# Cross attention in two layers: the context norm's scale and shift put into the key and value weights, the split of the context moved between engines, the keyless test rewritten, buffers doubled, and the written-out order replaced

## The reference, cut to what matters

```python
# layer 0: causal attention of x on the first 112 context rows that tril lets through
Q = relu(queries @ Wq.T + bq); K = relu(keys @ Wk.T + bk); V = relu(values @ Wv.T + bv)
scores = Q_ @ K_.T / 4
key_mask = sign(abs(sum(keys, -1)));  scores = where(key_mask == 0, NEG, scores)
scores = where(tril == 0, NEG, scores)
out = softmax(scores) * query_mask @ V_ + queries
x = gamma * (out - mean) / (std + EPS) + beta
# layer 1: causal self attention, cross attention on the whole context, and a feed-forward part
result = tgt + selfattention(ln1(tgt)) @ sa_wproj + sa_bproj
xq = ln(result) * ln2_g + ln2_b
xs = ln(src) * ln2_g + ln2_b            # src: the context, 375 rows of each batch
k2, v2 = split(xs @ ed_wkv)
result += softmax(xq @ ed_wq @ k2.T * scale) @ v2 @ ed_wproj + ed_bproj
result += relu(ln3(tgt) @ ff_w1 + ff_b1) @ ff_w2 + ff_b2
```

## Time and profile before

| | |
|---|---|
| three runs | 398.64, 398.82 and 401.52 us |
| median | 398.82 us |
| the profiled execution's own time | 397.9 us |
| its span, first to last instruction | 396.1 us |
| granted TensorE clock, mean | 0.978 of full |
| busy: PE, PEld | 336.6 us (85%), 269.4 us (68%) |
| busy: DVE, ACT, POOL | 242.8 us (61%), 171.4 us (43%), 69.6 us (18%) |
| DMA | 13.48 MB, mean 34 GB/s |

### The profile page before, as it was taken

One profiled execution on the slowest core, in us unless ns is written; L12 is line 12 of the kernel. 1 busy time (PEld: TensorE's weight loads), 2 busy tenths in 40 slices (PEclk: granted clock), 3 DMA queues, 4 the chain that ended last, 5 costly groups with the idle time before them and its releaser, 6 DMA issues.

```text
span 396.1 us, 10338 instructions
## 1 busy us (share of the span) xinstructions
PE 336.6 (85%) x4450; PEld 269.4 (68%) x4450; DVE 242.8 (61%) x574; ACT 171.4 (43%) x293; POOL 69.6 (18%) x77
## 2 busy tenths in 40 slices
PE   2787888998898988889989998998896999777995
PEld 2565666976686776667677775787674688565874
DVE  4786798765658665767856644297757741635311
ACT  1337445356532165532457344636071167333340
POOL 2023453131420011012102002532050110100000
PEclk9989969999999999999999999999989999989999
DMA  6783001100000004000000000010000000000001
GB/s 192 188 335 119 6 21 64 40 2 2 2 23 2 2 7 141 6 1 25 2 2 3 2 3 2 25 62 17 2 2 2 0 2 3 2 2 2 2 3 46
DMA packets 4249, 13.48 MB, mean 34 GB/s; under 512 B 518, under 2 KB 1654, under 8 KB 3947
## 3 DMA queue, kind: packets, MB, share of 16 engines
q1 hardware_dynamic: 3928, 12.72, 9.7%
q10 hardware_dynamic: 276, 0.10, 0.1%
HBM read 11.89 MB, written 0.92 MB: 32 GB/s over the span
## 4 chain that ended last, share of the span: by engine, by line
PE 63%; DVE 19%; ACT 8%; issue 4%; DMA 4%; POOL 1%; SPq 0%; DVEq 0%; ACTq 0%
PE ring L495 33%; PE ring L729 6%; ACT exps L838 6%; DVE negmax L993 6%; DVE negmax L967 5%; PE ring L616 4%; PE ring L744 4%; PE ring L596 4%; PE ring L590 3%; PE ring L628 3%; PE acc L641 2%; DMA xk_t<-in_xk_t 2%; DMA w_qk<-in_w_qk 2%; PE ring L608 1%; DVE v L1130 1%
## 5 line engine op out<-in xcount | busy, mean ns | idle before, releaser
L993 DVE TENSOR_REDUCE negmax<-ring 112x2 f32<-112x750 f32 x64 | 57.1, 935 | 16.3 <-PE ring L729 15.2
L838 ACT ACTIVATE exps<-ring 125x896 f32<-125x896 f32 x48 | 41.4, 915 | 26.7 <-PE ring L744 26.7
L1214 POOL TENSOR_SCALAR_AFFINE_SELECT exps<-exps 112x896 f32<-112x896 f32 x32 | 31.4, 1005 | 100.4 <-ACT exps L838 100.4
L967 DVE TENSOR_REDUCE negmax<-ring 112x8 f32<-112x896 f32 x32 | 33.4, 1086 | 18.5 <-PE ring L596 18.5
L838 ACT ACTIVATE exps<-ring,pad 112x896 f32<-112x896 f32 x32 | 30.5, 1005 | 25.3 <-PE ring L628 25.3
L641 PE MATMUL acc<-exps,v 125*17 125x112 f32 (+1 forms) x1280 | 39.6, 264 | 1.1 <-POOL exps L1214 0.5
L729 PE MATMUL ring<-k,q 32*112 32x376 f32 x384 | 24.8, 357 | 14.1 <-DVE negmax L993 8.6
L641 PEld LDWEIGHTS acc<-exps,v 125*17 125x17 f32 (+1 forms) x1280 | 28.6, 98 | 8.8 <-issue 4.7
L729 PEld LDWEIGHTS ring<-k,q 32*112 32x112 f32 x384 | 15.1, 169 | 21.8 <-issue 19.4
L495 PE MATMUL ring<-w_b,h 128*112 128x256 f32 x128 | 29.4, 383 | 0.0
L616 PE MATMUL ring<-maxrows,sel 32*125 32x224 f32 (+1 forms) x320 | 19.5, 316 | 9.1 <-ACT exps L838 2.6
(11 more groups left out here) (139 smaller groups left out, 591.8 us busy)
## 6 DMA issues: line engine op xcount, KB each, us to landing
c_nat<-in_ctx SPq DMA_DIRECT2D x4, 750.0 KB
w_b<-in_w_b SPq DMA_DIRECT2D x1, 2304.0 KB, 9.7
xk_t<-in_xk_t SPq DMA_DIRECT2D x4, 448.0 KB, 4.3
w_a<-in_w_a SPq DMA_DIRECT2D x1, 1280.0 KB, 6.0
xh<-in_keys SPq DMA_DIRECT2D x4, 224.0 KB, 4.7
x_nat<-in_x SPq DMA_DIRECT2D x4, 224.0 KB, 2.6
out<-x SPq DMA_DIRECT2D x4, 224.0 KB, 2.4
w_qk<-in_w_qk SPq DMA_DIRECT2D x1, 512.0 KB, 6.3
```

The lines of the kernel that those rows point to most:

```text
L838: return nc.scalar.activation(exps[0:k, EXP_AT[job], :, :], o[0:k, :, 0:4 * T], ACT.Exp, bias=bias)
L967: v_max[b].step(nc.vector.tensor_reduce(negmax[0][:, slot(g, b), 2 * m_:2 * m_ + 2, :], o[0:T, :, 0:4 * T].rearrange("p r (j t) -> p r j t ...
L993: x_max[b].step(nc.vector.tensor_reduce(negmax[1][:, b, 2 * m_:2 * m_ + 2, i], o[0:T, :, 0:S], AX.X, ALU.max, negate=True), g, 2 * i + m_ + 1)
L1214: p_masked[b].step(nc.gpsimd.affine_select(e, e, [[0, 8], [1, T]], ALU.is_ge, 0.0, base=0, channel_multiplier=-1), g, k)
```

## The change

- The rows of the key and value weights are multiplied by ln2_g on the chip while they are split: ScalarE writes the rounded part (`weights_hi`), VectorE the remainder (`weights_lo`). GpSimd has no part in it any more.
- A new step `shift`: TensorE multiplies ln2_b with the unscaled weights, and ScalarE copies the results to `shift_k` and `shift_v`. They are added when the keys (`key2`, `key2_rest`) and the values (`values2`) are read from the ring; the keys now in two instructions on each engine.
- `cT`: ScalarE copies the transposed context from the ring straight to the rounded part (`context_hi`, one instruction), VectorE subtracts that from the ring for the remainder (`context_lo`). `ct_tmp` and GpSimd's step are gone. The home of `cT` is free when VectorE is done, where it was free when ScalarE was.
- The keyless test: the first keys lie on eight partitions, VectorE sums and compares, and TensorE counts (`flag`, a step of its own).
- `masks` keeps the three readings of the counts; a new step `late` does the rest, and the update of `x_nat`.
- `xk_t` and `h` are doubled; the rings of `spread` and `acc_sb` go from two to three. The second `xk_t` is loaded at the start.
- `MIX` is new, and `rows` and `flag` stand first in it.

```diff
-MIX = ("AANRAAACDWREDCWPNEDEPEIDCIPJDCCPIJDICDCJPIAPAIAJCJPHCJJHIDEPCEDEPDAPICJDCDAJIPAIEJAAPAKFABJFPBIFJIBKFAEBHFBNEBPBBEBBFAAE"
-       "CEFBNDFBFDFCBPCFBFBPYFYDPHFCFCDPFKBEBEBFCKDBCDBDBPBFEAIBJEBAAFPDFFFDIADFCDFDYIJCYCIJPCIJCJPAHIJIHJAEAPEEAJPIEJIJPAIPJBKB"
-       "FIFFJIFKBPEBHBFEBPBBBBFEBEFEPBBFBPFFBFBFBYBPBBBFBFFBFHFPFKBFFFFFYFYKY")
+           "W": [("split", i) for i in range(PIECES)] + [("shift",)], "N": [(n, g) for g in GROUPS for n in ("keys", "masks", "late")],
+           "R": [("rows", i) for i in range(2)], "L": [("flag",), ("general",)]}
+MIX = ("RRLAALNNCENDECDNWWCADPCINCPEJWJICPNIDDCDJPPPDIJIJAPAJAIIPHHJPDEPACEEDCPCDCIDCDJEAIJAJAPKAIAHBBABJBIFJIFKFABEFEBPBBFNPCEP"
+       "BBEFEDBBNFFDCNFPDFPCABNHBFBFNEBCYPFYFEBFDFCDBKBFBBBFBCDCDANJAIAPDABCPFFDCFFCJFIDCIPDCDFAPAAKAJAPYEBYBJBIBJIHHBIPJBIKJPBK"
+       "FEBBEEFPBJEPIHJIPJBIPFIFBJIJEFPEEFPFFEFEHBFBFBBFKYBFPBBBFFFBFBBFKBFFFFFFYYY")
...
-RING = {step: i % 2 for steps in (SPREADS, COPIES) for i, step in enumerate(steps)}
+RING = {step: i % 3 for steps in (SPREADS, COPIES) for i, step in enumerate(steps)}
...
-        unsplit = h[:, :, :, :].rearrange("p f b t -> p (f b t)")[:, 0:C * 2 * U].rearrange("p (c u) -> p c u", c=C)
+        unsplit = h[1][:, :, :, :].rearrange("p f b t -> p (f b t)")[:, 0:C * 2 * U].rearrange("p (c u) -> p c u", c=C)
...
             load_queries(0)
+            load_x(1)
             sp.wait_ge(v0_loaded, 16)
             load_context(0)
-            sp.wait_ge(x_loaded[0], 16)
+            sp.wait_ge(xk_loaded[1], 16)
             load_keys(1)
...
+            def flag():
+                pe.wait_ge(prep_dve, PREP_DVE)
+                pe.wait_ge(flag_steps, 2)
+                nc.tensor.matmul(gen_s[:, 0:1], first_masked[:, :], ones[0:B, :], start=True, stop=True, skip_group_check=True).then_inc(flag_counted, 1)
...
+            def shifts():
+
+                o = claim(pe, ("shift",))
+                pe.wait_ge(kv_loaded, 16)
+                pe.wait_ge(flat_loaded, 16)
+                for i in range(C):
+                    products([(unsplit[:, ci, 128 * i:128 * (i + 1)], vec[:, VEC["b2"] + ci:VEC["b2"] + ci + 1]) for ci in range(C)], o[:, 0, i:i + 1], start=i == 0)
+                end(products([(vec[:, VEC["b2"] + ci:VEC["b2"] + ci + 1].to_broadcast([128, CH]), unsplit[:, ci, U:2 * U]) for ci in range(C)], o[0:CH, 1, 0:U]))
...
-            def context(g, b):
+            def context_hi(g, b):
                 if g or b:
-                    act.wait_ge(*p_ct_lo.at(g, b))
-                o = is_filled(act, ("cT", g, b))
-                for c in range(C):
-                    a_ct.step(nc.scalar.activation(ct_tmp[:, c, 0:S], o[:, c, 0:S], ACT.Identity, bias=col("b2")(c), scale=col("g2")(c)), g, 2 * b + c + 1)
+                    is_filled(act, ("v2", g, b - 1) if b else ("v2", g - 1, G - 1))
+                a_ct.step(nc.scalar.activation(ct[:, HI, :, 0:S], is_filled(act, ("cT", g, b))[:, :, 0:S], ACT.Copy), g, b + 1)
...
+                for i in range(C):
+                    a_k2.step(nc.scalar.activation(k2[g % 2][:, HI, b, i, :], o[:, i, 0:SP], ACT.Identity, bias=shift_k[:, i:i + 1]), g, C * b + i + 1)
+
+            def weights_hi(i):
+                if i == 0:
+                    act.wait_ge(kv_loaded, 16)
+                nc.scalar.activation(wkv2[:, HI, i, :], unsplit[:, i, :], ACT.Copy, scale=col("g2")(i)).then_inc(split_hi, 1)
...
-            def context_hi(g, b):
-                if g or b:
-                    is_filled(dve, ("v2", g, b - 1) if b else ("v2", g - 1, G - 1))
-                dve.wait_ge(*a_ct.at(g, 2 * b + 2))
-                v_ct_hi.step(nc.vector.tensor_copy(ct[:, HI, :, :], ct_tmp[:, :, :]), g, b + 1)
+            def context_lo(g, b):
+                o = is_filled(dve, ("cT", g, b))
+                dve.wait_ge(*a_ct.at(g, b + 1))
+                v_ct.step(nc.vector.tensor_tensor(ct[:, LO, :, 0:S], o[:, :, 0:S], ct[:, HI, :, 0:S].bitcast(F32), ALU.subtract), g, b + 1)
...
+                for i in range(C):
+                    hi, lo = (k2[g % 2][:, part, b, i, :] for part in (HI, LO))
+                    v_k2.step(nc.vector.scalar_tensor_tensor(lo, o[:, i, 0:SP], shift_k[:, i:i + 1], hi.bitcast(F32), ALU.add, ALU.subtract), g, C * b + i + 1)
...
-                v_v2.step(nc.vector.tensor_copy(v2[g % 2][:, b, :, :, 0:D], o[0:CH, :, :].rearrange("p j n -> p (j n)")[:, 0:NCH * U].rearrange("p (n h d) -> p n h d", n=NCH, h=H)), g, b + 1)
+                v_v2.step(nc.vector.tensor_tensor(v2[g % 2][:, b, :, :, 0:D], sums_, shift, ALU.add), g, b + 1)
...
+            def weights_lo(i):
+                dve.wait_ge(split_hi, i + 1)
+                nc.vector.scalar_tensor_tensor(wkv2[:, LO, i, :], unsplit[:, i, :], vec[:, VEC["g2"] + i:VEC["g2"] + i + 1], wkv2[:, HI, i, :].bitcast(F32), ALU.mult, ALU.subtract).then_inc(split_lo, 1)
...
+            def flag():
+                dve.wait_ge(first_loaded, 16)
+                nc.vector.reduce_sum(first_sum[:, :], first_keys, AX.X).then_inc(flag_steps, 1)
+                dve.wait_ge(flag_steps, 1)
+                nc.vector.tensor_scalar(first_masked[:, :], first_sum[:, :], 0.0, None, ALU.is_equal).then_inc(flag_steps, 1)
...
-            def context_lo(g, b):
-                pool.wait_ge(*v_ct_hi.at(g, b + 1))
-                p_ct_lo.step(nc.gpsimd.tensor_tensor(ct[:, LO, :, :], ct_tmp[:, :, :], ct[:, HI, :, :].bitcast(F32), ALU.subtract), g, b + 1)
```

183 lines of the change are left out of this document (90 added, 93 removed).

## The result

The changed kernel takes 386.83 us (median of 4 runs, 386.68 to 387.10), the kernel before 398.73 (4 runs beside it, 396.02 to 401.52): ratio 0.970, 95% interval 0.964 to 0.977. The profiled execution took 386.72 us for a span of 384.7, 11.4 less than the span of before.

The account below looks back on a forecast made before the run. The prediction took TensorE's work plus its 59.5 us of idle time to bound the kernel. Its terms, -0.5 + 1.2 - 2.0 + 0.5 - 1.5 + 0.4 + 0.8 - 0.2 = -1.3, gave 397.5 us, range 389.5 to 404.5.

Parts of the forecast that it names:

- start: At the kernel's start: bias rows hidden under the weights' load and no `xk_t` wait, -2.0 us (-3.5 to +0.5).
- the stretch after it: Second 20 us of TensorE work: VectorE has 25.5 us of work against TensorE's 20.1, +1.5 us (-1 to +5).
- close pairs: Distances between cross scores: 13 of 31 under 1 us, 12 before, +0.4 us (-3 to +4), standing for the middle.
- +0.8: At the end: copies of `acc` and `o_t` left bare, the `o_nat` wait covered, +0.8 us.
- idle time until 58 us of work are done: Early TensorE idle time, a sign of the forecast: over 17 us.
- idle time from 80 to 380 us: TensorE idle time in the middle 300 us: forecast wrong if under 33 or over 41 us.
- the mean clock: TensorE's granted clock over the kernel: forecast wrong if its mean leaves 0.97 to 0.99.
- Shift and flag: Sixteen more matmul instructions on TensorE, which nothing hides: +1.2 us (+0.8 to +2).
- GpSimd's cost: VectorE instructions lengthened beside GpSimd's work, half of 4.2 us counted as saved: -2.0 us (-4 to 0).
- -1.5 for `M`: Waits of `M` and `cM` for spread maxima, 6.0 us before: wider distances save 1.5 us (-3 to 0).
- Homes held longer: Ring homes of `cT` and `k2` freed later, over 16 fillings of three pairs: +0.5 us (0 to +4).
- The rival of 391.5: Middle 300 us: doubled buffers let steps stand where no reader is late, closing 5.9 us of idle; chance 0.34.

Follow-up runs that it names:

- old_split: Changed kernel with context and weights split as before, GpSimd's subtractions included, keys copied in one instruction per engine, no shift step: 394.75 us, ratio 0.987.
- before_rows_and_load: Kernel before with `rows` 0 and 1 in front of `q0` and two `xk_t` buffers, the second loaded at the start: 400.13 us, ratio 1.002.
- old_split_shift: Changed kernel with context and weights split as before, the shift step kept but its result unused: 394.00 us, ratio 0.989.
- pool_busy: Changed kernel plus an unread 624-column GpSimd subtraction at each of the eight `cT` steps: 389.19 us, ratio 0.971.
- new_until_142: Changed kernel with the new order up to the second `cT` of group 1, the old order from there: 396.10 us, ratio 0.994.
- single_h: Changed kernel with two buffers for `spread` and `acc_sb`, one for `h`, and `h` 0 of group 1 behind group 0's last `f`: 391.77 us, ratio 0.983.
- rings_of_two: Changed kernel with two buffers for `spread` and `acc_sb` in place of three: 385.45 us, ratio 0.965.
- old_order: Changed kernel in the order of before, `flag` behind the first `k0`, `late` behind `masks`, `shift` behind the second `split`: 410.78 us, ratio 1.019.
- rows_late_only: Changed kernel with `rows` 0 behind the first `k0` and `rows` 1 behind the second, `flag` left before `q0`: 390.88 us, ratio 0.978.
- rows_late: Changed kernel with `rows` 0 and `flag` behind the first `k0`, `rows` 1 behind the second: 392.44 us, ratio 0.984.
- before_filled: Kernel before with unneeded TensorE products inside four waits that falls of the clock had followed: 398.99 us, ratio 0.997.
- warm_start: Changed kernel with ten unneeded products ahead of the bias rows: 390.00 us, ratio 0.979.
- warm_short: Changed kernel with four unneeded products ahead of the bias rows: 387.63 us, ratio 0.972.
- warm_rings: Changed kernel with four unneeded products ahead of the bias rows and two buffers for `spread` and `acc_sb`: 387.81 us, ratio 0.971.

## Why the prediction was wrong

By the cut at equal steps, the 11.4 us of span come as 5.9 in the first 110 us, 6.5 between 142 and 365, with 0.1 given back between the two and 0.9 at the end. The terms that belong to these stretches were -0.5 (start, and the stretch after it), -1.1 (close pairs and `M`) and +0.8; the others, -0.5 in sum, are spread over the kernel. So two groups of terms failed, by some 5 us each. The signs that the prediction had set for itself say the same: idle time until 58 us of work are done is 12.3 us (forecast over 17), idle time from 80 to 380 us is 30.6 (wrong if under 33), and the mean clock is 0.991 (wrong if over 0.99).

**Right.** The method's frame held: the kernel's time is TensorE's work plus its idle time, and the change touches the idle time. `q0` came at 8.92 (forecast 9.2), no wait for `xk_t` is left, busy times and GpSimd's share came out, `late` and the end came out (tail +0.9 for +0.8: its waits of 0.76 and 0.63 us for ScalarE's copies are there as written). The 2.01 us outlier of `dev` is gone (0.41 to 0.42 in all eight), and so is that of the cast. The subtraction from PSUM took 938 ns (taken as 941), the keys' remainder 602 a piece. The stretch in which nothing else moved, 110 to 142 us, gave nothing.

**The two terms put at -0.5 together (start -2.0, the stretch after it +1.5): measured -5.9 by 110 us.** Two steps failed. The first: I let VectorE's excess of work in the second 20 us turn into TensorE's idle time at the rate of before, and took `M`'s distance as given. It did not: old_split shows that the changed way of the context is itself worth 3.1 us by 44 and 6.8 by 101 in this order, the falls of the clock included, which the forecast had booked elsewhere at -2.0 for the whole kernel. The second: no term had the clock. The kernel before loses 80 times 0.06, 4.8 us, to it by 80 us, the changed kernel nothing. I had priced one fall at 2.5 us, as a risk for the new order alone; that the falls of before could go was in no case. The split of the weights, 2.5 us on GpSimd, I had priced by the lengthening of VectorE and not by its place ahead of the first `M`, where the rows show 1.5 (before_rows_and_load). The bias rows came out at a bigger price than I gave (6.1 us of slow products for 3.3) and it cost nothing, since the weights' load and `flag` cover them.

**Shift and flag, +1.2: not on the path.** "Nothing hides work on the bounding engine" was the wrong step. TensorE bounds on the whole, but the shift's 2.2 us stand ahead of `M` of group 1, where TensorE waits 0.97 us even so. In old_split, without it, that wait is 2.98, and old_split_shift, with it, is no slower than old_split (394.00 and 394.75 us). Work on the bounding engine is free where that engine is going to wait. The size was off too: the shift took 2.2 us for 1.0, since its eight products of one column, put at little, took 1.05.

**GpSimd's cost, -2.0 (-4 to 0): too small in what it covered.** pool_busy gives 2.4 us with overlapping intervals, so the term for the lengthening of VectorE is about right. What it left out is the chain from `cT` to `k2`, shorter by some 1.8 us, the masking queued behind the subtraction, and the clock's share (loss 10.6 us for 3.4). I had dropped the chain because no wait of TensorE named the context step. That is true of the old order, which had room around it; the new one doesn't, and there old_split waits 3.0 us for `ct` and 2.2 for the masking. A wait that is absent in the order of before says nothing of the order after.

**Close pairs, +0.4 (-3 to +4) and -1.5 for `M`: measured -6.5 from 142 to 365 us.** This miss is as large as the one of the start. The count of close cross scores (12 and 13) was right in what it says: the waits for their maxima stayed at 8.1 us in this stretch. The term for `M` had the right sign and was too small: the waits for the spread maxima fell by 2.4 us here, with the 2.3 us wait gone. The step that failed is that these two counts stood for all of the middle's idle time. Most of the 7.0 us of idle time that went lies in pairs that were never counted, self maxima, `xh`, values, exponentials. new_until_142 puts 8.3 us of idle time on the order of these steps. The rival of 391.5 had that mechanism, and its 5.9 us ("a third of the gap") were near the size; 386.83 lies below it because of the start, which it didn't touch. Of its reasons, doubled `h` is shown to carry the order at one place (4.9 us, single_h), doubled `xk_t` nothing by itself (before_rows_and_load), the third buffers nothing (rings_of_two).

**Homes held longer, +0.5 (0 to +4): not told apart by a run.** TensorE now waits 1.6 us in 2 waits for `ct` and 1.1 in 3 for the keys' remainder, 2.7 in all, at steps that fill those homes again; the like in the kernel before was 0.6 (`ct_tmp`). So the term was too small, inside its range.

**How the pieces add.** They don't. The changed code in the old order is slower than before (1.9%, some 8 us, with three steps badly placed), the old split in the new order 5 us faster, the changed code in the new order 12 faster. A part's worth depends on the other part's being there. I had summed terms each read from the old order, and that is the reason why a forecast of 1.3 and a result of 11.9 both rest on right rows.

**What stays open.** How much of the 8.3 us each exchanged pair is worth. Why the clock falls at one wait and not at another of the same length: in the changed kernel three waits of 1.1 us in a row come ahead of the one fall, and like waits elsewhere have none. How much of old_order's loss are the three steps' places. And the mean gain by the clock: the same first steps had a fall at 42 us in new_until_142 and none in the changed kernel. The changed kernel is also built with a smaller scratch for DMA descriptors (`dynamic_dma_scratch_size=1024`), which the section on the change does not list; all variants of it have that too, and no run takes it out. before_rows_and_load has it as well, and gained nothing.

## What to carry to other kernels

Two orders of the same steps can't be told apart by counting the kinds of pairs that wait most now; walk both orders step by step, and give every reader between TensorE steps (norms, copies, splits) its time, the short ones too. In this kernel, bound by one engine's program order, an early delay was hardly caught up (6.1 us at 48 us were 5.8 at the end in rows_late_only, 7.3 were 5.2 in rows_late), so an early wait counts nearly in full, and work that was put in front of a remaining wait was free. Test a part of a change in the order that it will run in, since its worth in the old one may have the other sign. And look at the granted clock of more than the one execution that was traced: before_filled's trace showed the clock of its slower executions.

## What the hardware showed

- TensorE's first microseconds of work run at half pace, though the granted clock is printed as 1.00 there: the bias rows, with nothing before them, took 1.91 us for 1.02, and `q0` with `k0` behind them 5.29 for 3.29. After 7.4 us of other products (warm_start) they had full pace; after 3.7 us they had it in warm_short and not in warm_rings.
- Each fall of the clock had a loss of 1 to 4 us, near 1.2 GHz for 4 to 8 us (one of 14 us, loss 7, in old_order). In these traces most began behind a wait. Filling the waits ahead of four falls raised the mean clock in six of ten executions (0.987 and more, for 0.966 to 0.987 before) and moved the falls in the one that was traced; the median time stayed. Whether an order with fewer early waits has fewer falls isn't shown: the same first 142 us had one fall in new_until_142 and none in the changed kernel. TensorE, Matmul & The Clock Gate, in the Trainium skill, part 1, says that activity releases the throttle and idleness brings it back, and that the number of slow matmuls at the start varies from run to run. The traces agree with both: the 0.50 of full clock behind the waits in the changed kernel at 358 us, and 1.91 and 1.02 us for the same products in warm_rings and warm_short.
- A VectorE instruction of 0.40 us took 1.46 (pool_busy) beside a GpSimd subtraction of 1.51, and ended 0.15 us behind it. SBUF, State Buffer, in the Trainium skill, section "Who interferes with whom", calls the shared ports an exclusive lock for the whole instruction; the trace agrees. Its worth for the whole kernel was 2.4 us in the medians for eight such subtractions, 1.6 us in the trace without the fall of the clock.
